# Wide convolution-kernel steps on VectorE between its splits, one stack moved ahead of four evictions, and the first weight chunk in halves

## Time and profile before

| | |
|---|---|
| median of 3 runs | 204.57 us (203.69 to 205.06) |
| profiled execution | 203.41 us, span 201.5 us, mean granted TensorE clock 0.981 |
| TensorE matmul busy | 190.2 us, 94% of the span, 937 matmuls |
| VectorE busy | 117.8 us, 58% |
| ScalarE busy | 89.6 us, 44% |
| GpSimd busy | 95.5 us, 47% |
| TensorE in the chain that ended last | 92% |

### The profile page before, as it was taken

One profiled execution on the slowest core, in us unless ns is written; L12 is line 12 of the kernel. 1 busy time (PEld: TensorE's weight loads), 2 busy tenths in 40 slices (PEclk: granted clock), 3 DMA queues, 4 the chain that ended last, 5 costly groups with the idle time before them and its releaser, 6 DMA issues.

```text
span 201.5 us, 2654 instructions
## 1 busy us (share of the span) xinstructions
PE 190.2 (94%) x937; PEld 158.6 (79%) x937; DVE 117.8 (58%) x145; ACT 89.6 (44%) x142; POOL 95.5 (47%) x128
## 2 busy tenths in 40 slices
PE   7799999439999999999999999999999999999994
PEld 2388887327888888888877888888999999999994
DVE  0699854964705605605800831568989967677653
ACT  2554236610414973433316231286566656556500
POOL 6058889992000037197000000077959966766700
PEclk9999999958999999999999999999999999999999
DMA  6999970000000000000000330014888888887624
GB/s 208 339 364 428 423 293 0 0 0 0 0 3 0 2 0 2 3 0 0 0 0 7 91 127 0 0 44 135 225 291 288 301 269 297 265 274 237 246 108 156
DMA packets 14654, 27.33 MB, mean 136 GB/s; under 512 B 2450, under 2 KB 4914, under 8 KB 13746
## 3 DMA queue, kind: packets, MB, share of 16 engines
q1 hardware_dynamic: 13922, 25.79, 36.9%
q10 hardware_dynamic: 720, 1.38, 2.0%
HBM read 18.69 MB, written 8.47 MB: 135 GB/s over the span
## 4 chain that ended last, share of the span: by engine, by line
PE 92%; ACT 3%; DVE 2%; issue 2%; ACTq 0%
PE y_ps L561 12%; PE y_ps L562 12%; PE y_ps L563 12%; PE k_ps L625 10%; PE k_ps L627 10%; PE k_ps L626 10%; PE low_ps L555 4%; PE low_ps L556 4%; PE low_ps L557 4%; PE y_ps L568 3%; PE y_ps L576 2%; PE y_ps L584 2%; PE y_ps L580 2%; PE low_ps L534 2%; ACT x_all L467 1%
## 5 line engine op out<-in xcount | busy, mean ns | idle before, releaser
L420 POOL TENSOR_TENSOR t_lo<-w_raw,t_hi 128x512 fp32r<-128x512 f32 x32 | 45.7, 1440 | 51.1 <-ACT t_hi L481 51.0
L761 DVE COPY_PREDICATED low_sel<-lab_mask,low_ps 32x512 f32<-32x512 int32 x32 | 23.4, 731 | 46.9 <-PE low_ps L557 45.9
L625 PE MATMUL k_ps<-xs_hi,t_hi 128*128 128x128 f32 (+3 forms) x130 | 41.6, 320 | 0.2 <-DVE x_all L780 0.2
L627 PE MATMUL k_ps<-xs_lo,t_hi 128*128 128x128 f32 (+3 forms) x130 | 41.7, 321 | 0.0
L626 PE MATMUL k_ps<-xs_hi,t_lo 128*128 128x128 f32 (+3 forms) x130 | 41.5, 319 | 0.0
L561 PE MATMUL y_ps<-x_hi,w_hi 128*128 128x512 f32 x104 | 40.6, 391 | 0.0
L563 PE MATMUL y_ps<-x_lo,w_hi 128*128 128x512 f32 x104 | 40.6, 391 | 0.0
L562 PE MATMUL y_ps<-x_hi,w_lo 128*128 128x512 f32 x104 | 40.6, 390 | 0.0
L771 DVE TENSOR_TENSOR xs_lo<-x_all,xs_hi 128x512 fp32r<-128x512 f32 x32 | 30.3, 953 | 4.9 <-ACT xs_hi L475 4.9
L780 DVE COPY_PREDICATED x_all<-len_mask,k_ps 128x512 f32<-128x512 int32 x31 | 23.2, 748 | 11.8 <-PE k_ps L627 11.5
L467 ACT COPY x_all<-y_ps 128x512 f32<-128x512 f32 x30 | 16.6, 591 | 28.5 <-PE y_ps L568 28.5
(11 more groups left out here) (128 smaller groups left out, 219.5 us busy)
## 6 DMA issues: line engine op xcount, KB each, us to landing
w_raw<-k_pad SPq DMA_DIRECT2D x32, 256.0 KB, 4.2
out<-x_all SPq DMA_DIRECT2D x31, 256.0 KB, 3.6
x_all<-in_xt SPq DMA_DIRECT2D x7, 1024.0 KB, 12.8
w_raw<-in_wt ACTq DMA_DIRECT2D x4, 256.0 KB, 5.4
x_all<-in_xt SPq DMA_DIRECT2D x4, 256.0 KB, 7.1
ab_raw<-in_ab SPq DMA_DIRECT2D x1, 320.0 KB, 3.6
a_raw<-in_a_lab ACTq DMA_DIRECT2D x1, 320.0 KB, 7.5
out<-x_all SPq DMA_DIRECT2D x2, 128.0 KB, 1.7
```

The source lines that it names most:

```text
L420: g.tensor_tensor(t_lo[:, k % TR, :], t_raw[:, k % RAW, ::-1], f32(t_hi[:, k % TR, :]), ALU.subtract).then_inc(t_lo_done, 1)
L625: mm(o, t_hi[:, u, cols(lag)], xs_hi[:, b, x], start=(lag == 0), stop=False, skip_group_check=True)
L627: return mm(o, t_hi[:, u, cols(lag)], xs_lo[:, b, x], start=False, stop=ends, skip_group_check=True)
L761: v.copy_predicated(low_sel[:], lab_mask[rows, :].unsqueeze(1).to_broadcast([RANK, GH, P]), low_ps[rows, g % 2, :].rearrange("p (h b) -> p ...
```

## The change

1. GpSimd stops after the 128x32 quantities and signals `k_base`. The wide steps move to VectorE as three functions: `k_phases` (six steps, behind group 1's work), `k_wraps` (five steps, behind group 2's work, then `k_args`), and `k_scale` (six steps, behind group 4's work, when GpSimd has signalled `k_gains`; then `k_factors`). The reciprocal moves from group 4 to group 3. GpSimd keeps all 128x32 steps.
2. On ScalarE the stack of group 1 comes directly behind `x_hi` of group 2, ahead of the four evictions of group 0.
3. On VectorE the first half of group 2's `x_lo` moves into `select_low(1)`, ahead of the wait for the stack.
4. The first weight chunk is summed (VectorE) and cast (ScalarE) in two halves of 256 columns, and TensorE starts on the first half; `w_sum` and `w_hi_done` count one more.
5. On TensorE the four identity matmuls of the fold come ahead of the four `A0 B^T` matmuls, and wait for `consts` instead of the load.

```diff
-ACT_KGEN, DVE_KGEN, PE_KGEN = 3, 4, 5
+ACT_KGEN, DVE_KGEN, PE_KGEN = 3, 3, 5
...
+        def w_parts(c):
+            return ((1, slice(0, HALF)), (2, slice(HALF, L))) if c == 0 else ((c + 2, slice(0, L)),)
... (gpsimd)
-            outer(phase[:, q_at:u_at], turns[:], ramp_b[:], LB)
...
-            outer(mag[:, NQ:NQ + NP], re_dta[:], ramp_a[:], LA)
-            g.nop().then_inc(k_args, 1)
+            g.nop().then_inc(k_base, 1)
...
-            tt(q, q, mag[:, 0:NQ], ALU.mult)
...
-            g.tensor_tensor(u, u, v, ALU.add).then_inc(pool_own, 1)
-            pool.wait_ge(pool_own, own[0])
-            g.nop().then_inc(k_factors, 1)
+            g.nop().then_inc(k_gains, 1)
... (scalar)
-                act.wait_ge(w_sum, c + 1)
-                s.copy(w_hi[:, c, :], w_raw[:, c, :]).then_inc(w_hi_done, 1)
+                for n, o in w_parts(c):
+                    act.wait_ge(w_sum, n)
+                    s.copy(w_hi[:, c, o], w_raw[:, c, o]).then_inc(w_hi_done, 1)
...
-                stack_low(g)
+                if g != 1:
+                    stack_low(g)
                 if g == 0:
                     split_x_hi(2, 0)
                     split_x_hi(2, 1)
+                    stack_low(1)
... (tensor)
+            pe.wait_ge(consts, 2)
+            for c in range(CH):
+                mm(fold_ps[c][:, cols(c)], ident[:], ident2[:], start=True, stop=False, skip_group_check=True)
             pe.wait_ge(ab_load, 16)
             for c in range(CH):
                 r = slice(RANK * c, RANK * c + RANK)
-                mm(fold_ps[c], ab_raw[r, 0:P], ab_raw[r, P:P + L], start=True, stop=False, skip_group_check=True)
-            pe.wait_ge(consts, 2)
-            for c in range(CH):
-                mm(fold_ps[c][:, cols(c)], ident[:], ident2[:], start=False, stop=True,
+                mm(fold_ps[c], ab_raw[r, 0:P], ab_raw[r, P:P + L], start=False, stop=True,
                    skip_group_check=True).then_inc(folded, 1)
...
-                pe.wait_ge(w_hi_done, c + 1)
                 for d in range(CH):
+                    if c > 0 or d % 2 == 0:
+                        pe.wait_ge(w_hi_done, c + 2 if c > 0 else d // 2 + 1)
... (vector)
-                v.scalar_tensor_tensor(w_raw[:, c, :], fold_ps[c], LORA_SCALING, w_raw[:, c, :], ALU.mult, ALU.add)\
-                    .then_inc(w_sum, 1)
+                for _, o in w_parts(c):
+                    v.scalar_tensor_tensor(w_raw[:, c, o], fold_ps[c][:, o], LORA_SCALING, w_raw[:, c, o],
+                                           ALU.mult, ALU.add).then_inc(w_sum, 1)
... (select_low, behind the four copies)
+                if g == 1:
+                    split_x_lo(2, 0)
                 dve.wait_ge(lowst_hi, g + 1)
...
+            def k_phases():
+                dve.wait_ge(k_base, 1)
+                outer(phase[:, Q_AT:U_AT], turns[:], ramp_b[:], LB)
+                outer(phase[:, U_AT:V_AT], turns[:], ramp_a[:], LA)
+                ts(phase[:, V_AT:S_AT], phase[:, U_AT:V_AT], shift[:, 1:2], 1.0, ALU.add, ALU.mult)
+                ts(phase[:, Q_AT:V_AT], phase[:, Q_AT:V_AT], shift[:, 0:1], 1.0, ALU.add, ALU.mult)
+                ts(phase[:, S_AT:S_AT + H], turns[:], 0.5, 0.0, ALU.mult, ALU.add)
+                ts(phase[:, S_AT + H:], turns[:], 1.0, 0.0, ALU.mult, ALU.add)
+
+            def k_wraps():
+                ts(whole[:], phase[:], 1.0, ROUND, ALU.mult, ALU.add)
+                ts(whole[:], whole[:], 1.0, -ROUND, ALU.mult, ALU.add)
+                tt(phase[:], phase[:], whole[:], ALU.subtract)
+                outer(mag[:, 0:NQ], re_dta[:], ramp_b[:], LB)
...
+                v.tensor_tensor(mag[:, NQ:NQ + NP].rearrange("p (h n) -> p h n", n=LA),
...
+                v.nop().then_inc(k_args, 1)
+
+            def k_reciprocal():
+                dve.wait_ge(k_den, 1)
+                v.reciprocal(recip[:], tmp[:, 2, :]).then_inc(k_recip, 1)
+
+            def k_scale():
+                dve.wait_ge(k_gains, 1)
...
+                tt(q, q, mag[:, 0:NQ], ALU.mult)
+                tt(cu, cu, mag[:, NQ:NQ + NP], ALU.mult)
+                tt(cv, cv, mag[:, NQ:NQ + NP], ALU.mult)
+                by_head(cu, tmp[:, 9, :])
+                by_head(cv, tmp[:, 10, :])
+                v.tensor_tensor(cu, cu, cv, ALU.add).then_inc(k_factors, 1)
... (main loop of vector)
-                if 0 < g < GROUPS - 1:
+                if g == 1:
+                    split_x_lo(2, 1)
+                elif 1 < g < GROUPS - 1:
                     split_x_lo(g + 1, 0)
                     split_x_lo(g + 1, 1)
...
+                if g == 1:
+                    k_phases()
+                if g == 2:
+                    k_wraps()
                 if g == DVE_KGEN:
-                    dve.wait_ge(k_den, 1)
-                    v.reciprocal(recip[:], tmp[:, 2, :]).then_inc(k_recip, 1)
+                    k_reciprocal()
+                if g == DVE_KGEN + 1:
+                    k_scale()
```

More of the change, by code:

```diff
@@ L109, in conditioned_residual @@
         NQ, NP = H * LB, H * LA
+        Q_AT, U_AT, V_AT, S_AT = 0, NQ, NQ + NP, NQ + 2 * NP
         k_d = sb("k_d", [1, H, LA])
@@ L171, in conditioned_residual @@
         pool_own = sem("pool_own")
+        k_base = sem("k_base")
         k_args = sem("k_args")
+        k_gains = sem("k_gains")
         k_funcs = sem("k_funcs")
@@ L338, in _ @@
             ts(turns[:], turns[:], 1.0 / (2.0 * math.pi), 0.0, ALU.mult, ALU.add)
[L341 to L345, removed]
-            outer(phase[:, q_at:u_at], turns[:], ramp_b[:], LB)
[L347 to L355, removed]
-            outer(mag[:, NQ:NQ + NP], re_dta[:], ramp_a[:], LA)
-            g.nop().then_inc(k_args, 1)
+            g.nop().then_inc(k_base, 1)
             pool.wait_ge(k_funcs, 3)
-            tanh, sin_half, sin_one = half_a[:], phase[:, s_at:s_at + H], phase[:, s_at + H:]
-            q = phase[:, q_at:u_at]
-            u, v = phase[:, u_at:v_at], phase[:, v_at:s_at]
+            tanh, sin_half, sin_one = half_a[:], phase[:, S_AT:S_AT + H], phase[:, S_AT + H:]
             T = [tmp[:, i, :] for i in range(12)]
@@ L649, in _ @@
             pe.wait_ge(x_lo_done, CH)
-            pe.wait_ge(w_sum, CH)
+            pe.wait_ge(w_sum, CH + 1)
             for c in range(CH):
@@ L718, in split_chunk @@
                                 f32(x_hi[:, 0:GH, cols(c)]), ALU.subtract).then_inc(x_lo_done, 1)
-                dve.wait_ge(w_hi_done, c + 1)
+                dve.wait_ge(w_hi_done, c + 2)
                 v.tensor_tensor(w_lo[:, c, :], w_raw[:, c, :], f32(w_hi[:, c, :]), ALU.subtract)\
@@ L772, in split_xs_lo, with ts, tt, outer @@
                                 ALU.subtract).then_inc(xs_lo_done, 1)
+            def ts(o, i, s1, s2, op0, op1):
+                step(v.tensor_scalar(o, i, s1, s2, op0, op1))
+            def tt(o, a, b, op):
+                step(v.tensor_tensor(o, a, b, op))
+            def outer(o, col, ramp, n):
+                tt(o.rearrange("p (h n) -> p h n", n=n), col.unsqueeze(2).to_broadcast([P, H, n]),
+                   ramp.unsqueeze(1).to_broadcast([P, H, n]), ALU.mult)
+            def k_phases():
[6 more added lines that the diff above has]
+                ts(phase[:, S_AT + H:], turns[:], 1.0, 0.0, ALU.mult, ALU.add)
@@ new lines, in k_wraps @@
+            def k_wraps():
[3 more added lines that the diff above has]
+                outer(mag[:, 0:NQ], re_dta[:], ramp_b[:], LB)
+                own[0] += 1
+                v.tensor_tensor(mag[:, NQ:NQ + NP].rearrange("p (h n) -> p h n", n=LA),
+                                re_dta[:].unsqueeze(2).to_broadcast([P, H, LA]),
+                                ramp_a[:].unsqueeze(1).to_broadcast([P, H, LA]), ALU.mult).then_inc(dve_own, 1)
+                dve.wait_ge(dve_own, own[0])
+                v.nop().then_inc(k_args, 1)
@@ new lines, in k_reciprocal, with by_head @@
+            def k_reciprocal():
[3 more added lines that the diff above has]
+                dve.wait_ge(k_gains, 1)
+                q, cu, cv = phase[:, Q_AT:U_AT], phase[:, U_AT:V_AT], phase[:, V_AT:S_AT]
+                def by_head(o, col):
+                    o = o.rearrange("p (h n) -> p h n", n=LA)
+                    tt(o, o, col.unsqueeze(2).to_broadcast([P, H, LA]), ALU.mult)
+                tt(q, q, mag[:, 0:NQ], ALU.mult)
[4 more added lines that the diff above has]
+                v.tensor_tensor(cu, cu, cv, ALU.add).then_inc(k_factors, 1)
```

## The result

The changed kernel takes 195.44 us (median of 4, 194.75 to 195.58) against 204.58 for the kernel before: ratio 0.9551, 95% interval 0.9511 to 0.9591. On another chip it gave 195.83 against 203.88, ratio 0.9611 (0.9585 to 0.9636). The forecast was 195.9, in a range of 194.6 to 198.0. The profiled execution took 195.38 (span 193.3), 8.03 less than the profiled one of before; the forecast sum was 8.2.

A forecast was written before the change was run, and what follows sets the result against it. TensorE's matmuls were taken to bound the kernel, except its start and one idle before group 2's low-rank matmuls. 7.82 + 0.4 = 8.2 us off 203.41 (profiled) or 204.57 (median) gives 195.2 or 196.4; forecast 195.9, range 194.6 to 198.0.

The forecast's parts named there:

- The hole and the half clock: TensorE idle before group 2's low-rank matmuls (6.12 us) and the 0.61 clock behind it (1.70): 7.82 saved.
- Two causes: Group 2's x_lo on VectorE was late by queueing behind group 1's stack part and by taking 8.47 us instead of 2.36.
- The slow pair: Group 2's two x_lo steps on VectorE took 8.47 us because of GpSimd's wide steps; rival denying this: 197.3 or 199, chance 0.05.
- `k_wraps` in its idle: On VectorE behind group 2's x_lo, 6.6 + 0.2 us fits the 7.77 idle; no stall, 0.2 at the near end.
- `k_den` and `k_scale` at nothing: VectorE's wait for k_den before group 4's selection (2.8 us left) and k_scale behind group 4's x_lo cost nothing.
- The start, -0.4: Halved first weight chunk: first matmul 0.46 us earlier, 0.4 arriving at group 0's low-rank matmuls; between -0.6 and -0.1.
- The identity matmuls, put at nothing: On TensorE ahead of the fold: taken as 0, at worst a loss of 0.27 us, at best a gain of 0.2.
- The base of the sum: Time the 8.2 us is taken from: profiled 203.41 (gives 195.2) or median 204.57 (gives 196.4); forecast set between.
- rival: Four: k_wraps overrunning mildly, 0.09; x_lo slow anyway, 0.05; TensorE's wait staying, 0.03; VectorE wide steps at GpSimd's price, 0.03.
- The far end of the unknown: VectorE's wide steps at GpSimd's 5.49 us each: k_wraps 19.4, TensorE idle 10.8 at group 3, 208.4 total; chance 0.03.

The follow-up runs named there:

- The filled hole: Kernel before, with 24 matmuls that nobody reads put ahead of TensorE's wait for group 2's x_lo: 201.68 us (201.61 to 201.75).
- the repeated execution: Profiled execution of the changed kernel, unaltered, run again on another chip with three variants of its start: median 195.83 us, ratio 0.9611 to the kernel before.

## Why the prediction was right, step by step

- **The hole and the half clock: right, and shown.** 7.82 was forecast from group 2's base at 48.02. It starts at 39.88, 8.14 earlier, of which 0.40 was gained at the start of this execution; 7.74 are the hole's. The filled hole priced the clock's share at 1.62 (forecast 1.70).
- **Two causes: right, but taking away either was enough.** The sum treated order and moved steps as one. They do not add: 196.1 and 195.7 alone, 195.4 (195.8 on another chip) together.
- **The slow pair was GpSimd's doing: right, but the price was misread.** The length of the hole hung on one meeting. I read 8.47 us as the price of GpSimd's wide steps; 1.2 us of delay on GpSimd, with all of those steps still there, brought the x_lo pair to 4.13 and the wait to 0.27.
- **`k_wraps` in its idle: right.** 1.25 and 1.26 for the two steps of one tensor, 2.36 for the subtraction, 0.87 of idle left. Of 7.77 that leaves 6.90 used, where 6.8 was forecast. The Trainium skill, page "VectorE: DVE Perf Modes", section "The perf-mode tier table", has the first kind at two elements a cycle and the second at one; by that rule, the trace agrees.
- **`k_den` and `k_scale` at nothing: right.** VectorE waited 5.04 ahead of the reciprocal and still 2.38 for group 4's selection (forecast 2.8 left); `k_scale` left 2.27 ahead of group 5's.
- **The start, -0.4: the term that failed.** This execution shows it (low-rank matmuls at 15.91 instead of 16.31), the medians do not: 195.83 with, 195.79 without. I took a_lo as the next limit and its time as fixed. It was the limit in the repeated execution, but at 16.38 instead of 15.82, because x of chunk 1 came late; such arrivals move from execution to execution by more than the 0.4. The identity matmuls, put at nothing, did not hide ahead of the fold: in both profiles of the changed kernel the fold begins at 4.70, right behind them, where it began at 4.39 before. That is near the worst case of the prediction, a push of twice 0.27, of which 0.27 is got back behind the fold.
- **The base of the sum: in part luck.** I put the forecast between the profiled execution and the median. The two profiled executions differ by 8.03, near the sum's 8.2, and 0.4 of that is a start that the medians do not show; the medians differ by 9.14 on this chip and 8.05 on another. What made the executions of before differ by 2 us is not shown: one alone was profiled, and time and mean clock do not go together (204.99 at 0.983, 203.72 at 0.981).

No rival came true. The far end of the unknown (5.49 a step) was off by a factor of two to four. Had it been right, it would have cost more than the gain: 7.1 us more on VectorE left 1.0 of it, and the prediction's 19.4 for `k_wraps` is 12.5 more than the 6.90 that it used.

## What to carry to other kernels

When one engine's step takes a multiple of its usual time, look for the step of another engine that it overlaps, and see whether it ends just behind that one's end: then the moment decides, and a small shift of either can be worth as much as moving the work. Two repairs of one stall do not add; time each alone before keeping both. An edit that brings a start forward is worth only what the next arrivals let through; compare the moment at which the steady work begins, and not the total times alone.

## What the runs showed of the hardware

- A VectorE step with two inputs in SBUF that met a wide GpSimd step (the second x_lo step) ended 1.06 to 1.09 after it in four traces (the kernel before, its changed start, its filled hole, its delayed GpSimd), whether that step had 2.8 or 5.5 us, and GpSimd's step is the longer one when VectorE came first (2.92 for 1.97). The Trainium skill, page "SBUF — State Buffer", section "Who interferes with whom", says that a VectorE instruction with two SBUF inputs contends with a GpSimd instruction that reads SBUF, calls the port pair that they share an exclusive lock, and lets the order of issue decide who blocks; by that rule, the trace agrees.
- The granted clock was down behind TensorE idles of 1.59 and 1.65 ahead of the first chunk (0.50), 1.94 (0.61 over the stretch) and 5.70 (0.54). It was 1.00 behind one of 0.97, behind one of 1.36 ahead of the first chunk in the kernel before, and behind the filled hole.
- The trace has two records for each of the four `A0 B^T` matmuls of the fold, in two rounds of four. The first round took 0.53 in the execution with the old fold order (4.20 to 4.73) and 1.02 in the repeated one with the old start (4.27 to 5.29), which has the same fold code. So the start moves by half a microsecond without any edit of it.
